# Attention and a mixture of experts on one core: small moves at attention's outer steps, a context load moved, and the experts' bounds read later

## The chip, the core and the metric

The kernel runs on one NeuronCore of a Trainium2 chip. A core has a matrix engine (TensorE, PE in the profile, with its weight loads as PEld), VectorE (DVE), ScalarE (ACT), GpSimd (POOL) and SyncE (SP), which here only issues transfers. The engines run on their own and wait for each other by semaphores. PSUM is the memory that TensorE writes; names that begin with `ps` are tiles in it. The metric is the device time of one execution in microseconds; lower is better.

## The reference, cut to what matters

The batch is 4, the sequence 1024, the width 1024, the context 1024 rows of 512. There are 32 experts with inner width 512, and each token goes to 4 of them. All tensors are float32.

```python
def _L0_xattn_ref(teacher_logits, teacher_features, Wq, bq, Wk, bk):
    query = jnp.einsum('bnc,dc->bnd', teacher_features, Wq) + bq
    key = jnp.einsum('bnc,dc->bnd', teacher_features, Wk) + bk
    energy = jnp.einsum('bnd,bmd->bnm', query, key)
    attention = jax.nn.softmax(energy, axis=-1)
    return jnp.einsum('bln,bmn->blm', teacher_logits, attention)
...
def _L0_ffn_ref(hidden_states, gate_w, gate_b, w_gate, b_gate, w_up, b_up, w_down, b_down):
    logits = x @ gate_w.T + gate_b
    topk_logits, topk_idx = jax.lax.top_k(logits, K)
    topk_weight = jax.nn.softmax(topk_logits.astype(jnp.float32), axis=-1)
    ...
    gate = jax.lax.ragged_dot(xt, w_gate, group_sizes) + b_gate[gid]
    up = jax.lax.ragged_dot(xt, w_up, group_sizes) + b_up[gid]
    gate = jnp.minimum(gate, SWIGLU_LIMIT)
    up = jnp.clip(up, -SWIGLU_LIMIT, SWIGLU_LIMIT)
    glu = gate * jax.nn.sigmoid(SWIGLU_ALPHA * gate)
    outs = jax.lax.ragged_dot((up + 1.0) * glu, w_down, group_sizes) + b_down[gid]
    ...
x = x + _L0_xattn_ref(_layernorm(x, axis=-1), ctx_1024, L0_xattn_Wq, L0_xattn_bq, L0_xattn_Wk, L0_xattn_bk)
x = x + _L0_ffn_ref(_layernorm(x, axis=-1), ...)
```

## The kernel before, in words

The program has two stages with a barrier between them: attention with routing (to about 640 us of the span), and the experts (to the end). Every large product is made of three float16 passes (high by high, high by low, low by high part), so that the result is close to float32. The order of the work on each engine is written out by hand; nothing is planned by a program.

**Attention.** Per batch, the context (2 MB, `cx`) is transposed in four pairs of tiles (`context`, L634), and the queries and keys are made from it in four quarters (`one_quarter`, L640), which VectorE reads out of PSUM with their bias (`queries_and_keys`, L850). Then there are eight tiles of 128 rows. `energies` (L609) fills `psE`; VectorE takes the row maximum (L860), ScalarE the exponent (L538); VectorE and ScalarE write the high and low parts of the probabilities (L545, L877) and of the normalised rows of x, and SyncE transposes both with DMA (L424, L429). A batch's second product (`product`, L676: 48 matmuls of 512 columns per tile, two halves of 24) runs one batch later than its energies. `schedule` lays out steps `step(s, b1, b2, more)`: b1 is the batch whose energies are made, b2 the one whose second product is made, s the tile, and `more` is False where b1 is past the last batch. So batch 0's energies stand alone (b2 is None), and the last batch's product stands alone (from `more` False at s = 0 and 1, then b1 None). I call these the outer steps; `both` is the step between them, in which the small matmuls (transposes of the second norm's rows L614, routing logits L623 into `psR`) stand between the large ones of the product.

In an outer step of the last batch TensorE makes the first half of the product, then 8 transposes into `psT`, 12 matmuls of the second half, the 8 logits matmuls, the last 12, and the two rank matmuls (L731, L732). The logits read `x2T`, which ScalarE copies out of `psT` (L578). The product goes to `psM` or `psE`: before, `psE` only where b1 is None and s is odd. VectorE adds the residual from it (L936).

**Between the stages** SyncE loads the first slot list (`idxg`, L457), GpSimd gathers the first 128 rows by it (`xg`, L510), and the barrier follows. SyncE also loads the first pieces of weights (`load_chunk`, L117).

**Experts.** Tokens are sorted into slots of 128 rows; an expert has 3 or more such tiles, and its last may be a half tile of 64 rows (`half_step`). Per tile, TensorE makes the gate product (`psG`, L1326), the transposes of the previous tile's activation (L1339), the up product (`psU`), the transposes of the next tile's rows (`psX`, L1332), and the previous tile's down product (`psY`, L1350): 24 matmuls each. After a half tile the down product is made in pairs of 64 rows that run together. ScalarE copies `psX` to `xT` (L1166) before the gate product can begin. The number of tiles is known only on the chip: an expert's first tile, its end of full tiles and its end are read into registers (`start_of` L1082, `full_end_of` L1085). `expert` reads all three at its start, behind the first tile's step of that expert, which the expert before has already issued.

```python
            def expert(e, par, last=False):
                t0, tf, t1 = start_of(pe, e), full_end_of(pe, e), start_of(pe, e + 1)
                ...
                with pe.Fori(t0 + 1, tf) as i:
                    step(i, e, par, False)
                with pe.If(t1 > tf):
```

## Time and profile before

| | |
|---|---|
| time, median of 3 runs | 3005.17 us (2998.52 to 3007.32) |
| time of the profiled execution | 3001.28 us |
| its span, first to last instruction | 2999.4 us |
| PE busy | 2887.7 us (96%) |
| DVE busy | 1705.9 us (57%) |
| ACT busy | 1193.8 us (40%) |
| POOL busy | 568.0 us (19%) |
| HBM traffic over the span | 156 GB/s |

The profile is one execution. Busy shares are of the span, and PE's leaves 112 us in which TensorE has nothing to do; the rows below say where they lie. The slices of the page show them at the start (0 to 100 us) and at the seam of the stages (600 to 675 us); elsewhere every slice is at 90% or more, but for the last.

### The profile page before, as it was taken

To read this page: it belongs to the slowest core of one execution; us is meant where nothing else is said; L and a number is where in the kernel's file an instruction comes from. 1 tells how busy PE (TensorE), PEld (TensorE's weight loads), DVE (VectorE), ACT (ScalarE), POOL (GpSimd) and SP (SyncE) were. 2 spreads that over 40 slices of the span, in tenths; PEclk is the share of its full clock that TensorE was granted. 3 is DMA by queue.
4 is the path that set the end of the run, shared out by engine and by line. 5 is a ranking of instruction groups with operands and counts; after the bars stand their busy time and mean duration, and the time that the engine had idled before them with its cause. 6 is when DMAs were issued, how large, how long until landed. Compare 5 with 4: busy or idle time off the path is not lost.

```text
span 2999.4 us, 44819 instructions
## 1 busy us (share of the span) xinstructions
PE 2887.7 (96%) x14948; PEld 1488.7 (50%) x14949; DVE 1705.9 (57%) x2552; ACT 1193.8 (40%) x1221; POOL 568.0 (19%) x502
## 2 busy tenths in 40 slices
PE   6899999959999999999999999999999999999997
PEld 3455555535454454444545444444544444455453
DVE  5887888654635454656554556655554654653532
ACT  3343333223524434544443445534444443442422
POOL 1132333321111111111111111211111111111111
PEclk8999999979999999999999999999999999999999
DMA  7977766555655555566755656766555665664433
GB/s 220 224 209 180 189 169 176 184 172 151 186 144 161 161 161 161 165 182 192 217 133 133 212 167 168 210 210 168 165 166 159 168 166 161 168 192 126 84 64 64
DMA packets 343547, 501.47 MB, mean 167 GB/s; under 512 B 190881, under 2 KB 190881, under 8 KB 343234
## 3 DMA queue, kind: packets, MB, share of 16 engines
q0 software_dynamic: 45856, 152.33, 22.9%
q10 hardware_dynamic: 94576, 225.46, 21.5%
q1 hardware_dynamic: 203058, 122.94, 15.9%
q8 instruction: 33, 0.54, 0.1%
q14 instruction: 24, 0.20, 0.0%
HBM read 354.64 MB, written 112.46 MB: 156 GB/s over the span
## 4 chain that ended last, share of the span: by engine, by line
PE 74%; DMA 2%; issue 1%; ACT 0%; DVE 0%; ACTq 0%; SPq 0%; POOL 0%; POOLq 0%; DVEq 0%
PE psY L1350 23%; PE psG L1326 22%; PE psU L1326 21%; PE psX L1332 4%; PE psG L1397 3%; PE psA L1339 2%; DMA acc<-y,idxs 1%; DMA idxs<-slots 1%; DMA bias<-in_L_ffn_b_down 0%; ACT y L1176 0%; ACT W L1073 0%; DVE y L1248 0%; SPq L1095 0%; ACT xT L1166 0%; ACTq L1092 0%
## 5 line engine op out<-in xcount | busy, mean ns | idle before, releaser
L1350 PE MATMUL psY<-W,aT 128*128 128x512 f16 (+1 forms) x3456 | 728.5, 379 | 3.0 <-DVE y L1248 3.0
L1326 PE MATMUL psG<-W,xT 128*128 128x512 f16 x3072 | 685.2, 379 | 16.6 <-issue 10.7
L1326 PE MATMUL psU<-W,xT 128*128 128x512 f16 x3072 | 684.1, 379 | 0.0
L1350 PEld LDWEIGHTS psY<-W,aT 128*128 128x128 f16 (+1 forms) x3456 | 321.1, 99 | 355.9 <-ACT aT L1170 3.3
L1326 PEld LDWEIGHTS psG<-W,xT 128*128 128x128 f16 x3072 | 299.7, 98 | 383.6 <-issue 21.3
L1326 PEld LDWEIGHTS psU<-W,xT 128*128 128x128 f16 x3072 | 299.3, 98 | 334.8
L1133 POOL DMA_INDIRECT acc<-y,idxs x143 | 229.4, 1604 | 1090.2 <-DVE y L1248 944.5
L1248 DVE SCALAR_TENSOR_TENSOR y<-psY,idxs,y 128x1024 f32<-128x1024 f32 x127 | 163.0, 1284 | 412.1 <-ACT y L1176 412.1
L676 PE MATMUL psM<-W,XT 128*128 128x512 f16 x1392 | 356.1, 379 | 5.8 <-DVE xr L936 5.2
L1176 ACT ACTIVATE y<-bias,idxs 128x1024 f32<-128x1024 f32 x143 | 164.3, 1149 | 464.5 <-DMA idxs<-slots 464.4
L1166 ACT ACTIVATE xT<-psX 128x1024 f32<-128x1024 f32 x145 | 148.3, 1023 | 461.7 <-PE psX L1332 436.6
L1128 POOL DMA_INDIRECT xg<-xn_tab,idxg x145 | 156.4, 1078 | 860.9 <-PE psX L1332 806.5
L1273 DVE SCALAR_TENSOR_TENSOR up<-psU,bias 128x512 f32<-128x512 f32 (+1 forms) x144 | 99.6, 692 | 278.5 <-PE psU L1326 278.0
L1262 DVE SCALAR_TENSOR_TENSOR gt<-psG,bias 128x512 f32<-128x512 f32 (+1 forms) x144 | 99.4, 690 | 261.1 <-PE psG L1326 205.2
L1078 DVE SCALAR_TENSOR_TENSOR W<-stage,W 128x2048 f16<-128x2048 f32 x93 | 212.4, 2284 | 9.1 <-ACT W L1073 9.1
L676 PEld LDWEIGHTS psM<-W,XT 128*128 128x128 f16 x1392 | 150.6, 111 | 126.9 <-DVE xr L936 6.9
L1078 DVE SCALAR_TENSOR_TENSOR W<-stage_more,W 128x2048 f16<-128x2048 f32 x93 | 212.4, 2284 | 1.2 <-ACT W L1073 1.2
L1170 ACT ACTIVATE aT<-psA 128x512 f32<-128x512 f32 x144 | 85.2, 592 | 263.5 <-PE psA L1339 255.8
L1073 ACT ACTIVATE W<-stage_more 128x2048 f16<-128x2048 f32 x93 | 176.3, 1896 | 34.7 <-issue 28.3
L1073 ACT ACTIVATE W<-stage 128x2048 f16<-128x2048 f32 x93 | 176.4, 1897 | 6.1 <-issue 5.9
L501 POOL DMA_INDIRECT slots<-pack,dest x128 | 138.2, 1079 | 200.1 <-DVE tok L912 162.3
L1332 PE MATMUL psX<-ident,xg 128*128 128x128 f32 x1160 | 152.1, 274 | 14.5 <-PEq L144 14.5
(170 smaller groups left out, 2616.7 us busy)
## 6 DMA issues: line engine op xcount, KB each, us to landing
stage_more<-in_L_ffn_w_down ACTq DMA_DIRECT2D x62, 1024.0 KB, 7.6
stage<-in_L_ffn_w_gate ACTq DMA_DIRECT2D x60, 1024.0 KB
stage_more<-in_L_ffn_w_up ACTq DMA_DIRECT2D x31, 1024.0 KB, 5.5
stage<-in_L_ffn_w_up ACTq DMA_DIRECT2D x30, 1024.0 KB
stage<-in_x SPq DMA_DIRECT2D x32, 512.0 KB
xr<-in_x SPq DMA_DIRECT2D x32, 512.0 KB
acc<-xr SPq DMA_DIRECT2D x32, 512.0 KB
xn_tab<-x2h SPq DMA_DIRECT2D x32, 512.0 KB
```

Of the source, the lines that this page charges most:

```text
L501: pool.indirect_dma_start(out=slots[:, :], out_offset=bass.IndirectOffsetOnAxis(dest[:, n % 2, k:k + 1], 0), in_=pack[:, n % 2, k, :], in_ ...
L676: op = pe.matmul(out[:, h * HALF:(h + 1) * HALF], XT[:, a, k, t * P:(t + 1) * P], AT[:, par(bk), c, k, h * HALF:(h + 1) * HALF].rearrange( ...
L1073: act.activation(W[:, par, HI, c * CHUNK:(c + 1) * CHUNK], slot(c), ACT.Copy, scale=S_W).then_inc(s_whi, 1)
L1078: dve.scalar_tensor_tensor(out=W[:, par, LO, c * CHUNK:(c + 1) * CHUNK], in0=slot(c), scalar=S_W, in1=W[:, par, HI, c * CHUNK:(c + 1) * CH ...
L1128: pool.indirect_dma_start(out=xg[:], out_offset=None, in_=xn_tab[:, :], in_offset=bass.IndirectOffsetOnAxis(idxg[:, 0:1].bitcast(U32), 0)) ...
L1133: pool.indirect_dma_start(out=acc[:, :], out_offset=bass.IndirectOffsetOnAxis(idxs[:, 0:1].bitcast(U32), 0), in_=y[:], in_offset=None, com ...
L1166: act.activation(xT[:].rearrange("p k q a -> p (k q a)").bitcast(F32), psX[:], ACT.Copy).then_inc(s_xTev, 1)
L1176: act.activation(y[:], bias[:, par, 2 * I:], ACT.Copy, scale=idxs[:, 1:2].bitcast(F32)).then_inc(s_y0, 1)
L1248: dve.scalar_tensor_tensor(out=tile_y[:], in0=psY[:], scalar=weight, in1=tile_y[:], op0=ALU.mult, op1=ALU.add).then_inc(s_y, 1)
L1326: op = pe.matmul(ps[:], xT[:, k, :, a], weights(par, c, offset + k * I, I), start=k == 0 and n == 0, stop=k == KH - 1 and n == 2)
L1332: op = pe.transpose(psX[:, n * P:(n + 1) * P], xg_w[:, n * P:(n + 1) * P], ident[:])
L1350: return pe.matmul(psY[at_row:at_row + rows, h * HALF:(h + 1) * HALF], aT[:, k, 0:rows, a], weights(par, c, 2 * KH * I + k * H + h * HALF, ...
```

## The change

- The first batch's context is loaded in four transfers of 0.5 MB, each with its own semaphore, and each pair of transposes waits for its own.
- Batch 2's context is loaded at step 1 of the next batch, behind the load of a residual tile, instead of at step 6 of batch 0.
- In batch 0's last step VectorE reads batch 1's queries and keys right after the low parts of tile 6, ahead of the statistics and the low parts of tile 7.
- At s = 0 and 1 of the last batch's product the outer step follows the rule of the others: odd tiles go to `psE`, and the product waits for the residual of the tile before the last one. In all of these steps the logits matmuls stand between those of the second half of the product, from its fifth on.
- At the seam SyncE loads the first slot list ahead of one piece of weights (w_up, stage slot 2), and ScalarE's copy of `xT` comes first, then the bias loads, then three loads of weights; before, the weights came first, then the bias, then the copy.
- In the experts' stage TensorE reads an expert's end behind its loop of full tiles. For an even expert the next one's end of full tiles is read there too, and the odd expert reads nothing at its start.

```diff
+            def load_first_ctx(pair):
+                rows = ctx_in[0, pair * 2 * P:(pair + 1) * 2 * P, :]
+                sp.dma_start(cx[:, 2 * pair:2 * pair + 2, :], rows.rearrange("(t p) c -> p t c", p=P)).then_inc(s_ctx0[pair], 16)
+
-            load_ctx(0)
+            for pair in range(NT // 2):
+                load_first_ctx(pair)
...
                 if b1 is not None:
+                    if s == 1 and b2 is not None and batch(b1) == 1:
+                        sp.wait_ge(s_cT, NT)
+                        load_ctx(2)
                     guarded(sp, more if s < 2 or s >= NT - 2 else None, next_x1)
                     guarded(sp, more if s < 2 else None, transposes)
-                    if s == NT - 2:
-                        guarded(sp, None if first(b1) else b1[0] < B - 3, next_ctx)
+                    if s == NT - 2 and not first(b1):
+                        guarded(sp, b1[0] < B - 3, next_ctx)
...
-                    if b1 is None:
+                    if b1 is None and s < NT - 1:
                         sp.wait_ge(s_wlo, s - 1)
                         g["load_chunk"](sp, 0, s - 2 + RING)
...
             sp.dma_start(g["idxg"][:], slots[0:P, :]).then_inc(g["s_idxg"], 16)
+            sp.wait_ge(s_wlo, NT - 2)
+            g["load_chunk"](sp, 0, NT - 3 + RING)
...
-        def product_of(s, b1):
-
-            return psE if b1 is None and s % 2 else psM
+        def product_alone(s, b1, more):
+
+            return b1 is None or s < 2 and more is False
+
+        def product_of(s, b1, more):
+
+            return psE if product_alone(s, b1, more) and s % 2 else psM
...
-                if pair == 0:
-                    alone(pe, s_ctx, per(16, bk, 16), s_past)
+                if first(bk):
+                    pe.wait_ge(s_ctx0[pair], 16)
+                elif pair == 0:
+                    pe.wait_ge(s_ctx, per(16, bk, 0))
...
-                    if b1 is None and s > 2:
+                    if product_alone(s, b1, more) and s > 0:
                         pe.wait_ge(s_exp, B * NT)
                         pe.wait_ge(s_x2, tile(b2, s - 1))
...
+                def logits_beside(m):
+                    if m == 4:
+                        pe.wait_ge(s_x2Tev, tile(bt, n + 1))
+                        if n >= 1 or not first(bt):
+                            pe.wait_ge(s_lgev, tile(bt, n))
+                    if 4 <= m < 4 + KH:
+                        logits_block(m - 4)
+
                 if b2 is not None and s < NT:
-                    product(product_of(s, b1), b2, s, 1, range(KH // 2))
-                if late:
-
-                    pe.wait_ge(s_x2Tev, tile(bt, n + 1))
-                    if n >= 1 or not first(bt):
-                        pe.wait_ge(s_lgev, tile(bt, n))
-                    for k in range(KH):
-                        logits_block(k)
+                    product(product_of(s, b1, more), b2, s, 1, range(KH // 2), logits_beside if late else None)
+                elif late:
+                    for m in range(4, 4 + KH):
+                        logits_beside(m)
...
                     if b2 is None and s > 0:
                         lo_parts(s - 1)
+                    if b2 is None and s == NT - 1:
+                        queries_and_keys(following(b1))
...
+            evac_x(0)
+            load_bias(act, 0, 0)
             for c in range(RING, NCHUNK):
                 load_chunk(act, 1, c)
-            load_bias(act, 0, 0)
-            evac_x(0)
...
-            def expert(e, par, last=False):
-
-                t0, tf, t1 = start_of(pe, e), full_end_of(pe, e), start_of(pe, e + 1)
+            def expert(e, par, known=None, last=False):
+
+                t0, tf = known or (start_of(pe, e), full_end_of(pe, e))
...
                 with pe.Fori(t0 + 1, tf) as i:
                     step(i, e, par, False)
+                t1 = start_of(pe, e + 1)
+                following = (t1, full_end_of(pe, e + 1)) if par == 0 else None
                 with pe.If(t1 > tf):
```

**VectorE, batch 0's last step.** `mx` is the row maximum of the last tile, `ah` and `xnh`/`xg` are the low parts, `stage<-ps..,bqk` the four readings of batch 1's queries and keys, BN_STATS the statistics of the tile's rows. Before:

```order
L860 TENSOR_REDUCE mx<-psE 128x1 [waits energy_done]
L861 TENSOR_SCALAR nmx<-mx 128x1 [waits softmax_chain]
L877 SCALAR_TENSOR_TENSOR ah<-stage,sc,ah 128x1024 [waits prob_scale_ready,prob_hi]
L880 SCALAR_TENSOR_TENSOR xnh<-stage,xnh 128x1024 [waits ln1_hi]
L821 BN_STATS st<-stage 128x6 [waits x1_in1]
L821 BN_STATS st<-stage 128x6
L823 BN_AGGR mv<-st 128x2 [waits ln1_chain]
```

Now, with the change:

```order
L881 TENSOR_REDUCE mx<-psE 128x1 [waits energy_done]
L882 TENSOR_SCALAR nmx<-mx 128x1 [waits softmax_chain]
L900 SCALAR_TENSOR_TENSOR ah<-stage,sc,ah 128x1024 [waits prob_scale_ready,prob_hi]
L903 SCALAR_TENSOR_TENSOR xnh<-stage,xnh 128x1024 [waits ln1_hi]
L871 TENSOR_SCALAR stage<-psM,bqk 128x512 [waits qk_done]
L871 TENSOR_SCALAR stage<-psQ,bqk 128x512 [waits qk_done]
L871 TENSOR_SCALAR stage<-psM,bqk 128x512 [waits qk_done]
L871 TENSOR_SCALAR stage<-psR,bqk 128x512 [waits qk_done]
L842 BN_STATS st<-stage 128x6 [waits x1_in1]
```

The four readings moved ahead of the statistics; before they came seven instructions later, behind the low parts of tile 7.

**TensorE, the last batch's product at s = 1.** `xs` are the normalised rows whose transposes go to `psT`, `psR` the logits, `psQ` the ranks. Before:

```order
L676 MATMUL psM<-W,XT 128x512 [waits ln1T_in1,x2_ready]
L676 MATMUL psM<-W,XT 128x512 x23
L614 MATMUL psT<-ident,xs 128x128 [waits ln2_ready]
L614 MATMUL psT<-ident,xs 128x128 x7
L676 MATMUL psM<-W,XT 128x512 x12
L623 MATMUL psR<-gateT,x2T 128x32 [waits logits_read,ln2T_evacuated]
L623 MATMUL psR<-gateT,x2T 128x32 x7
L676 MATMUL psM<-W,XT 128x512 x12
```

Now (the pair of a product's and a logits matmul goes on until there are eight logits):

```order
L693 MATMUL psE<-W,XT 128x512 [waits ln1T_in1,x2_ready,exp_done]
L693 MATMUL psE<-W,XT 128x512 x23
L629 MATMUL psT<-ident,xs 128x128 [waits ln2_ready]
L629 MATMUL psT<-ident,xs 128x128 x7
L693 MATMUL psE<-W,XT 128x512 x4
L638 MATMUL psR<-gateT,x2T 128x32 [waits logits_read,ln2T_evacuated]
L693 MATMUL psE<-W,XT 128x512
L638 MATMUL psR<-gateT,x2T 128x32
L693 MATMUL psE<-W,XT 128x512
```

The product's tile changed from `psM` to `psE`, and the wait of the logits for `x2T` (ln2T_evacuated) now stands behind 4 matmuls of the second half, before behind 12.

**TensorE's sequencer, from an even expert to its loop of full tiles and out of it.** Each TENSOR_LOAD reads a bound into a register. Before, the odd expert's start (the branch waits for that expert's weights):

```order
L1421 UNCONDITIONAL_BRANCH [waits weights_lo]
L1082 TENSOR_LOAD tile_start
L1082 ISA x2
L1085 REGISTER_ALU
L1085 TENSOR_LOAD full_end
L1085 ISA x2
L1082 ISA
L1082 TENSOR_LOAD tile_start
L1082 ISA x2
L1416 ISA
```

Now, behind the last full tile's down product of the even expert:

```order
L1373 MATMUL psY<-W,aT 128x512 x23
L1439 REGISTER_ALU
L1439 COMPARE_AND_BRANCH
L1105 ISA
L1105 TENSOR_LOAD tile_start
L1105 ISA x2
L1108 REGISTER_ALU
L1108 TENSOR_LOAD full_end
L1108 ISA x2
L1443 COMPARE_AND_BRANCH
```

The three reads at the odd expert's start are gone; the even expert has two at its end (and two instead of three at its start), the odd one has one.

## Rows read from the trace of the kernel before

**Rows 1.** Waits of PE from 640 us: us in total, times, longest us.

```profile
PE psG L1326 <- issue: 10.7, 15, 1.2
PE psG L1326 <- ACT xT L1166: 5.9, 3, 3.1
```

**Rows 2.** Timeline, start: start us, us, instruction, count [idle before <-releaser].

```profile
14.06 1.94 PE L634 MATMUL psM<-ident,W 128*128 128x128 f32 x8 [7.67 <-DMA W<-in_ctx]
...
21.56 7.13 PE L640 MATMUL psM<-W,WT 128*128 128x512 f32 x16 [1.11 <-ACT W L521]
```

**Rows 3.** Timeline, batch 0's last steps and the turn to batch 1.

```profile
83.26 1.98 PE L609 MATMUL psE<-stage 128*128 128x512 f32 x4 [1.48 <-ACT stage L538]
...
88.83 3.47 SPq L424 DMA_TRANSPOSE W<-ah  x1
...
89.85 1.28 DVE L821 BATCH_NORM_STATS2 st<-stage 128x6 f32<-128x512 f32 x2
...
95.58 0.74 DVE L850 TENSOR_SCALAR stage<-psM,bqk 128x512 f32<-128x512 f32 x1
96.12 8.89 SPq L424 DMA_TRANSPOSE W<-ah  x1
...
98.44 3.49 PE L609 MATMUL psE<-stage 128*128 128x512 f32 x4 [6.33 <-DVE stage L850]
101.77 10.82 PE L676 MATMUL psM<-W,XT 128*128 128x512 f16 x48
```

**Rows 4.** Timeline, the last batch's product at s = 0 and 1, and s = 3.

```profile
511.31 2.75 PE L676 MATMUL psM<-W,XT 128*128 128x512 f16 x12
...
511.51 1.02 ACT L578 ACTIVATE x2T<-psT 128x1024 f32<-128x1024 f32 x1 [1.40 <-PE psT L614]
...
513.90 1.87 PE L623 MATMUL psR<-gateT,x2T 128*128 128x32 f32 x16
...
518.20 0.30 PE L731 MATMUL psQ<-mask,before 128*128 128x32 f32 x2
...
519.75 5.35 PE L676 MATMUL psM<-W,XT 128*128 128x512 f16 x24 [1.03 <-DVE xr L936]
...
547.57 5.34 PE L676 MATMUL psE<-W,XT 128*128 128x512 f16 x24
```

**Rows 5.** Timeline of PE, a step that has logits between the product's matmuls.

```profile
434.24 0.38 PE L676 MATMUL psM<-W,XT 128*128 128x512 f16 x1
...
434.60 0.38 PE L676 MATMUL psM<-W,XT 128*128 128x512 f16 x1
```

**Rows 6.** Timeline, the seam of the two stages.

```profile
635.63 0.96 POOL L501 DMA_INDIRECT slots<-pack,dest  x1 [0.31 <-issue]
...
639.03 0.38 SPq L117 DMA_DIRECT2D stage<-in_L_ffn_w_up  x1
639.59 0.38 SPq L457 DMA_DIRECT2D idxg<-slots  x1
644.65 0.98 POOL L510 DMA_INDIRECT xg<-xn_tab,idxg  x1 [8.05 <-DMA idxg<-slots]
...
650.18 1.94 PE L1332 MATMUL psX<-ident,xg 128*128 128x128 f32 x8 [14.47 <-PEq L144]
...
655.22 6.66 PE L1326 MATMUL psG<-W,xT 128*128 128x512 f16 x24 [3.09 <-ACT xT L1166]
```

**Rows 7.** Transfers of the same slot list's kind: KB each, median us to landing.

```profile
idxs_last<-slots SPq DMA_DIRECT2D x1, 2.0 KB, 2.4
```

**Rows 8.** Reads of an expert's bounds, 812.7 to 815 us: ns min/median/max, start us.

```profile
L1082 PEldq TENSOR_LOAD <-tile_start x2: 298/298/299, 812.8 to 814.3; - x2
```

**Rows 9.** Timeline of PE, two experts' starts behind a half tile.

```profile
811.43 2.78 PE L1350 MATMUL psY<-W,aT 128*64 128x512 f16 x24
815.38 5.34 PE L1326 MATMUL psG<-W,xT 128*128 128x512 f16 x24 [1.17 <-issue]
...
926.67 5.34 PE L1326 MATMUL psG<-W,xT 128*128 128x512 f16 x24 [0.49 <-issue]
```

More of the change, by code:

```diff
@@ L230, in attention_and_routing @@
         s_ctx = sem("ctx_in")
+        s_ctx0 = [sem(f"first_ctx_in{pair}") for pair in range(NT // 2)]
         s_past = sem("waits_passed")
@@ L757, in step @@
                     inputs_landed(b2, s, 0)
-                    product(product_of(s, b1), b2, s, 0, range(KH))
+                    product(product_of(s, b1, more), b2, s, 0, range(KH))
                     inputs_landed(b2, s, 1)
@@ L784, in step @@
                 if b2 is not None and s < NT:
-                    product(product_of(s, b1), b2, s, 1, range(KH // 2, KH)).then_inc(s_xm, 1)
+                    product(product_of(s, b1, more), b2, s, 1, range(KH // 2, KH)).then_inc(s_xm, 1)
                 if b1 is not None:
@@ L935, in step @@
                     dve.wait_ge(s_xm, tile(b2, s + 1))
-                    dve.scalar_tensor_tensor(out=xr[:, s % 2, :], in0=product_of(s, b1)[:], scalar=1.0 / (S_ROWS * S_PROB),
+                    dve.scalar_tensor_tensor(out=xr[:, s % 2, :], in0=product_of(s, b1, more)[:], scalar=1.0 / (S_ROWS * S_PROB),
                                              in1=xr[:, s % 2, :], op0=ALU.mult, op1=ALU.add).then_inc(s_x2, 1)
@@ L943, in step @@
                         g["cut_lo"](dve, 0, 0, s - 3)
-                if b1 is not None and s == NT - 1:
+                if b1 is not None and b2 is not None and s == NT - 1:
                     guarded(dve, more, lambda: queries_and_keys(following(b1)))
@@ L1422, in expert @@
                     then(P)
+                return following
             pe.sem_inc(s_Y, 1)
@@ L1428, in _ @@
             with pe.Fori(0, PAIRS - 1) as pair:
+                known = None
                 for par in range(2):
-                    expert(pair * 2 + par, par)
-            expert(E - 2, 0)
-            expert(E - 1, 1, last=True)
+                    known = expert(pair * 2 + par, par, known)
+            known = expert(E - 2, 0)
+            expert(E - 1, 1, known, last=True)
 _INS = ["x", "ctx_1024", "L0_xattn_Wq", "L0_xattn_bq", "L0_xattn_Wk", "L0_xattn_bk", "L0_ffn_gate_w", "L0_ffn_gate_b",
```

## The prediction, made before the changed kernel ran

> **What bounds the kernel now.** I read the page first: TensorE is busy for 96% of the span, so a change pays where TensorE stands still or where its own work shrinks. Then I read the waits of PE, to see who ends its idle time. In the experts' stage the largest group, 10.7 us in 15 waits before the gate product, ends by "issue": no other engine is late there [rows 1]. Then the timeline at each place that the edits touch: the start [rows 2], the turn from batch 0 to batch 1 [rows 3], the last batch's product [rows 4], the seam of the stages [rows 6], and two experts' starts [rows 9]. Each is taken below as a time on TensorE's path, and I ask what is late next.
>
> **Start.** TensorE waits 7.67 us for the whole context and begins at 14.06; four groups of transposes and their copies later, at 21.56, the queries and keys begin: 7.5 us [rows 2]. With the load in four pieces, the last piece lands about when the whole did, and the first three groups are done by then. What stays is one group, 1.94, and the wait for its copy, 1.11 [rows 2]: 3.05 instead of 7.5, so 4.5 us saved. Three further issues on SP delay the loads behind them, which are wanted only after the queries and keys. Upper bound 5.1 (the group at full clock: the eight transposes of 0.11 us instead of 0.24 each), lower bound 0, if four small transfers land so much later than one large one.
>
> The Trainium skill, page "DMA: Bandwidth & Descriptors", section "Bandwidth", says to batch transfers to 1 MiB or more, with 2.0 us of fixed cost in its fit. By that, charged to each piece one after the other, the last would land some 6 us later and the start would lose 1.5 us (an estimate from the page). The trace of before has only the one large load here and does not settle it; the fixed cost should overlap when issues follow each other, so I keep the 4.5.
>
> **The turn to batch 1.** Before, the statistics of tile 7 begin at 89.85, the readings of the new queries and keys only at 95.58, and TensorE, idle since 98.44 - 6.33 = 92.11, makes the first energies at 98.44 [rows 3]. Now three readings run from about 90, and the fourth right after 92.11 and ends at 92.9 (0.74 each, [rows 3]): energies at 93.1, 5.3 us earlier. What is late next is tile 7's probabilities. Its statistics start at 92.9 instead of 89.85, so everything behind them moves 3.1 us back. Before, the two low parts ended where the readings began, at 95.58, and the probabilities' one, which the transpose needs, one pass or about 1.1 us sooner, at 94.5; now 97.6. Before, SP was at the context load then: it issued the transpose at 96.12 and took 8.89 us, against 3.47 for the tile before [rows 3]. With the context load gone it is through at 97.7 + 3.5 = 101.2 instead of 105.0. The product's 48 matmuls lasted 10.82, only 0.45 over 48 of 0.216, so its second half began at 107.1, 2.1 us after that issue was through [rows 3]. Now: 103.3, 3.8 us earlier, with a new wait of TensorE of 3 us between the halves (100.1 to 103.3), released by the transpose. Moving the context load back to step 1 costs the same 5.4 us of SP there, but the transposes and loads behind it are for tiles a full step and more away, and the context itself (about 10 us to land) has the whole of step 1; I cost it at 0, and at 3 if it lands after the first transposes of step 2.
>
> The clock takes some of it back: the four passes of a tile's energies took 3.49 us after the idle 6.33, and 1.98 after an idle 1.48 [rows 3], so after long idle time TensorE runs at 1.2 instead of 2.4 GHz. The 3 us hole may cost a few us of half clock, at half their length. I take 0.7, bounds 0 and 1.7 (8 matmuls at twice 0.216). So 3.1 us here, between 1 and 5.
>
> The page "TensorE: Matmul & The Clock Gate", section "HAM oscillation", of the Trainium skill says that idle gaps between bursts return the clock to half. The slow energies agree with that. By the rule at its worst the turn would give 2.1 us instead of 3.1.
>
> **Last batch's product.** At s = 1 and s = 2 the product waits for VectorE to read `psM`: 1.03 us each, of the same kind. The rank matmuls start at 518.20 and the product at 519.75, 1.55 later; four rank passes need some 0.35 of that. At s = 3, in the other PSUM tile, there is no wait [rows 4]. So 2 x 1.2 = 2.4 us saved. Next late would be the normalised rows for the transposes; the steps from s = 3 on already run at this pace. Bounds 1.5 and 2.4.
>
> **Logits joined to the product.** Apart, the cluster of logits costs 1.71: it starts at 513.90, behind 12 matmuls from 511.31 (12 x 0.216 = 2.6), and lasts 1.87 less the overlap of its end [rows 4]. Joined, product plus logits take 0.36 per pair [rows 5] against 0.216 alone: 8 x 0.14 = 1.14 us. That looks like 0.57 saved in each of eight steps. But the logits need `x2T`, which is ready at 512.53 [rows 4], and they now stand behind 4 matmuls, at 511.31 + 0.86 = 512.17. So 0.4 to 0.5 of waiting comes in, and the first logits pair, its weights not yet loaded, costs some 0.1 more: 1.7 against 1.7. I cost the eight steps at 0, bounds -3 (copy late when ScalarE is busy) and +4.5 (8 x 0.57). This edit is the most visible in the code, and I expect nothing of it.
>
> **Seam.** The slot list is issued at 639.59, behind a 1 MB load issued at 639.03, and the gather that waits for it starts at 644.65 [rows 6]: 5.1 us for 2 KB. A load of the same size elsewhere lands in 2.4 [rows 7]. The last scatter of slots is issued at 635.63 [rows 6]; I take about 2 us for its landing, so the list goes out at 637.8 and the gather at 640.2. That is 4.4 us earlier; sharing the queues with the 1 MB load, now issued while the gather runs, costs 0.1 at least and up to 2. I take 4.3, bounds 2 and 5. Then ScalarE's copy: the transposes end at 652.12, and the gate product starts at 655.22 after an idle 3.09 [rows 6], since ScalarE issues six transfers first. A copy of that size takes 1.02 [rows 4], with its two hand-overs 1.3: 1.8 saved. The bias, no longer behind 3 MB of weights, lets VectorE and ScalarE start tile 0 earlier, and of the remaining 2.8 us of waits for `xT` [rows 1] I take 0.6. The gate product at the seam ran its first matmuls at half clock (6.66 for 24, against 5.34 in [rows 9]); starting 2 us closer to the idle stretch can cost 0.5. Sum 4.3 + 1.8 + 0.6 - 0.5 = 6.2.
>
> **Experts.** The loss is behind half tiles only. A down product of 64 rows, run in pairs, is over in about 2.6 us (12 x 0.216), and the gate product could follow at 811.43 + 2.6 = 814.0; it starts at 815.38, so 1.3 is lost, 1.17 of it as idle time [rows 9]. Of the 15 waits [rows 1], seven are such, at even experts (0.97 to 1.17), and an eighth of 1.0 is put down to `xT`; six are of 0.49, at odd ones, and the last two experts have 0.5 and 0.15. TensorE's sequencer is then still reading bounds: one at 812.8, the third at 814.3 [rows 8], so 0.75 each. Odd experts lose 0.49 of idle [rows 9] and about 0.17 that the modelled ends hide, as do all the others. Now the even ones save one read, 8 x 0.75 = 6.0; the odd ones everything, 6 x 0.66 = 4.0; the last two 0.95; in one even case `xT` is ready only halfway, less 0.3. Sum 10.7, bounds 8 and 12. The reads come back behind the loop of full tiles, two at even experts and one at odd ones, up to 1.6 us, and what hides them is a down product at full length, 24 x 0.216 = 5.2. Three reads behind such a product leave no idle time today: all 15 waits are behind half tiles.
>
> **Sum.** 4.5 + 3.1 + 2.4 + 0 + 6.2 + 10.7 = 26.9. The profiled execution took 3001.28 (span 2999.4): 2974.4. The median of the runs is 3.9 above it: 2978.3. I say 2976.
>
> **Rivals.**
> (a) Only what lies behind no transfer pays: four pieces land late, the transpose holds the turn, the gather is slowed. Then experts 10.7, outer steps 2.4, 1.8 of the seam: 14.9, 2989 by the same mean. For it: all three rest on landings that the trace of before does not show. Against: 3.47 against 8.89 and 5.1 against 2.4.
> (b) The logits joined do gain 0.57 a step, 4.5 in all: 2971.5. Against it stands the 512.53 of `x2T`.
> (c) Slower: the reads behind the loop are not hidden. The price is 16 x 2 x 0.75 at even and 15 x 0.75 at odd experts, 35 us, against 26.9 of gain: 3011. It decides from when the sequencer is less than about 2.4 us ahead of TensorE at the end of a full down product (1.6 of reads and the branches). Against it: with three reads, 2.25 us, there is no gap behind full products.
> (d) The gaps are filled but the time is not: another engine is at its pace right behind. 3000. Against it: DVE and ACT are far from full in the experts' stage.
>
> **Numbers.** Chances: forecast 0.62, (a) 0.18, (b) 0.10, (c) 0.04, (d) 0.06. The likeliest's own range, from the bounds of its terms not all at one end, is 2968 to 2984. With (a) and (b) and the spread of 9 us between the runs shown: 2964 to 2990. About 0.3%, 9 us, is what can be told from no change. Faster 0.90, within 0.06, slower 0.04.
>
> **What would show it.** Right: TensorE's queries and keys begin near 17; the first energies of batch 1 run 5 us earlier in their turn, and a new wait of TensorE on `W<-ah` stands in the product's middle; waits before the product on `xr` vanish at s = 1 and 2; each logits cluster gone but a new wait on `x2T` of 0.4; the gather at the seam within 5 us of the last scatter; "issue" before the gate product under 4 us in all. Wrong: issue gaps in front of the transposes L1339 or the gate product behind full tiles, context transposes of batch 2 that wait for their load, or queries and keys still at 21.

## The result and the profile after

The changed kernel takes **2974.06 us** (median of 6, 2973.77 to 2975.55), against 3002.64 (median of 6) for the kernel before: ratio 0.9904, 95% interval 0.9892 to 0.9917. The forecast was 2976. The profiled execution has a span of 2972.2 us, 27.2 below the one before; the sum of the prediction was 26.9. That total is closer than its terms, so they are read one by one below.

The waits of TensorE from the seam on (us in total, times, longest), which answer to [rows 1]:

```profile
PE psX L1355 <- PEq L144: 11.1, 1, 11.1
PE psY L1373 <- DVE y L1271: 2.9, 2, 2.7
PE psG L1349 <- ACT xT L1189: 2.9, 3, 1.2
PE psG L1349 <- issue: 1.8, 7, 0.4
```

"Issue" has shrunk from 10.7 to 1.8 us, xT from 5.9 to 2.9, and nothing new has come in. The start, beside [rows 2]:

```profile
7.79 1.94 PE L651 MATMUL psM<-ident,W 128*128 128x128 f32 x8 [1.28 <-DMA W<-in_ctx]
...
12.81 1.04 PE L651 MATMUL psM<-ident,W 128*128 128x128 f32 x8
15.01 7.13 PE L657 MATMUL psM<-W,WT 128*128 128x512 f32 x16 [1.16 <-ACT W L536]
```

The last group of transposes starts at 12.81, though the last piece of the context had landed at 12.0: TensorE was still at the third group. Unlike the first two it runs at full clock (1.04 us). The queries and keys start 6.55 us earlier than before. The turn to batch 1, beside [rows 3]:

```profile
86.98 1.96 PE L624 MATMUL psE<-stage 128*128 128x512 f32 x4 [0.94 <-DVE stage L871]
88.78 5.34 PE L693 MATMUL psM<-W,XT 128*128 128x512 f16 x24
...
91.45 3.25 SPq L434 DMA_TRANSPOSE W<-ah  x1
...
96.21 5.34 PE L693 MATMUL psM<-W,XT 128*128 128x512 f16 x24 [2.10 <-DMA W<-ah]
```

The hole before the first energies is gone (0.94 instead of 6.33), a new one of 2.10 stands in the middle of the product, and the transpose takes 3.25 instead of 8.89. The long one has moved with the context load: at 114.18, 1.8 us behind that load, a transpose takes 9.62 us, and TensorE does not wait for it. The last batch's product, beside [rows 4]:

```profile
494.31 5.35 PE L693 MATMUL psM<-W,XT 128*128 128x512 f16 x24 [0.50 <-issue]
...
501.65 0.41 PE L638 MATMUL psR<-gateT,x2T 128*128 128x32 f32 x2 [0.25 <-ACT x2T L593]
507.56 5.34 PE L693 MATMUL psE<-W,XT 128*128 128x512 f16 x24
```

The wait on `xr` of 1.03 is gone at s = 1 (and at s = 2), and the first joined logits wait 0.25 for `x2T` in seven of the eight steps, 0.37 in the last. The seam, beside [rows 6]:

```profile
621.92 0.96 POOL L516 DMA_INDIRECT slots<-pack,dest  x1 [0.30 <-issue]
...
624.10 0.33 SPq L470 DMA_DIRECT2D idxg<-slots  x1
625.32 0.38 SPq L117 DMA_DIRECT2D stage<-in_L_ffn_w_up  x1
626.10 0.98 POOL L525 DMA_INDIRECT xg<-xn_tab,idxg  x1 [3.22 <-DMA idxg<-slots]
...
633.05 1.94 PE L1355 MATMUL psX<-ident,xg 128*128 128x128 f32 x8 [11.05 <-PEq L144]
```

The gather starts 4.18 us after the last scatter instead of 9.02, but TensorE's wait falls only from 14.47 to 11.05. The experts' starts behind a half tile, an even and an odd one, beside [rows 9] (a group that the view's window cuts shows fewer than 24 matmuls):

```profile
792.66 2.78 PE L1373 MATMUL psY<-W,aT 128*64 128x512 f16 x24
795.87 4.48 PE L1349 MATMUL psG<-W,xT 128*128 128x512 f16 x20 [0.42 <-issue]
...
903.88 2.78 PE L1373 MATMUL psY<-W,aT 128*64 128x512 f16 x24
906.59 5.35 PE L1349 MATMUL psG<-W,xT 128*128 128x512 f16 x24
```

At the odd one the gate product now follows 2.71 after the down product's start, with no idle time; at even ones 0.2 to 0.4 is left.

### The profile page after: what moved, and what is told of

It reads as the page before. It is cut to its first block, busy times and chain, and to the rows that moved or that the text cites. A ratio compares the mean times of both kernels' runs of the same rounds, so it can differ in the third digit from the quotient of the medians.

```text
span 2972.2 us, 44771 instructions
## 1 busy us (share of the span) xinstructions
PE 2885.2 (97%) x14948; PEld 1487.7 (50%) x14949; DVE 1705.2 (57%) x2552; ACT 1192.0 (40%) x1221; POOL 563.8 (19%) x502
## 3 DMA queue, kind: packets, MB, share of 16 engines
q10 hardware_dynamic: 94576, 225.46, 21.6%
## 4 chain that ended last, share of the span: by engine, by line
PE 76%; DMA 1%; ACT 0%; issue 0%; DVE 0%; SPq 0%; POOL 0%; ACTq 0%; POOLq 0%; DVEq 0%
PE psY L1373 23%; PE psG L1349 22%; PE psU L1349 22%; PE psX L1355 4%; PE psG L1420 3%; PE psA L1362 2%; DMA acc<-y,idxs 1%; DMA idxs<-slots 1%; ACT y L1199 0%; DVE y L1271 0%; ACT xT L1189 0%; SPq L1118 0%; ACT W L1096 0%; POOL acc L1180 0%; PE psU L1421 0%
## 5 line engine op out<-in xcount | busy, mean ns | idle before, releaser
L693 PE MATMUL psM<-W,XT 128*128 128x512 f16 x1344 | 349.2, 379 | 5.8 <-DVE xr L959 2.9
```

The costliest lines, as they stand in the source:

```text
L693: op = pe.matmul(out[:, h * HALF:(h + 1) * HALF], XT[:, a, k, t * P:(t + 1) * P], AT[:, par(bk), c, k, h * HALF:(h + 1) * HALF].rearrange( ...
```

## The experiments

Twelve kernels ran. Times are medians of the runs; the kernel before, run beside each group, took 3004.07, 3001.87 and 3003.08, so medians of two groups compare to 1 or 2 us. Where less matters, the stretch of the trace that the edit touches decides. "Changed" is the changed kernel, 2974.06.

**bounds_only**: the kernel before with `t0, tf = known or (...)` and the reads of `t1` and of the next expert's bounds behind `Fori`, and nothing else of the change.

> The kernel before with the experts' bounds edit alone: an expert's end and the next one's bounds read behind the loop of full tiles. Theory (the reads hide under a down product at full length, and what was lost was exposed behind half tiles): the waits of the gate product on issue, 10.7 us in 15 waits in the kernel before, fall under 2 us as in the changed kernel, and from the second gate product of the stage to the last down product TensorE gains 9.9 us, as the changed kernel did there: a span near 2989.5, ratio 0.9967. Rival 1 (the gain there was owed to the other edits, through the seam and the bias): a gain of 5 us or less. Rival 2 (the reads come back behind full tiles): new gaps before the activation's transposes, span at or above 2999.

2990.20 (4 runs), ratio 0.9950 (0.9934 to 0.9967). Waits of PE from 650 us:

```profile
PE psG L1326 <- ACT xT L1166: 4.5, 3, 2.6
PE psY L1350 <- DVE y L1248: 2.9, 1, 2.9
PE psG L1326 <- issue: 1.7, 7, 0.4
```

From the stage's second gate product to the last down product it takes 2300.3 us, the kernel before 2310.5, the changed kernel 2300.7. So the bounds edit alone is the whole gain of this stage, 10.3 us; rivals 1 and 2 fall. The medians differ by 13.9, with 5.8 between this kernel's own runs; the stretch is the better measure.

**more_reads**: four further `full_end_of(pe, e)` ahead of the read of `t1`.

> The changed kernel with four more reads of a bound behind each expert's loop of full tiles (six at even experts, five at odd ones; 0.75 us each). Theory (TensorE's sequencer is some 17 matmuls or 3.5 us ahead of the engine at the end of a full down product, and no more): 4.5 us of reads and the branch leave some 1.2 us exposed at 16 even experts, 3.75 us leave some 0.5 at 15 odd ones: 27 us more, between 15 and 40, as waits on issue before the activation's transposes or the gate product. Rival 1 (the whole down product of 5.2 us is cover): no more than 3 us. Rival 2 (reads behind the loop are never covered): 31 x 3.0 = 93 us more, and the changed kernel should already have shown it.

2995.40 (6 runs), 21.3 above changed; the stretch took 2323.0, 22.3 more. At even experts the hole comes behind a full down product, or before the half tile's transposes (7 waits of up to 0.9 us):

```profile
717.81 5.34 PE L1373 MATMUL psY<-W,aT 128*128 128x512 f16 x24
724.25 1.02 PE L1349 MATMUL psG<-W,xT 128*128 128x512 f16 x4 [1.10 <-issue]
...
1049.99 5.34 PE L1349 MATMUL psG<-W,xT 128*128 128x512 f16 x24 [0.88 <-issue]
```

Both rivals fall, and 22.3 lies within the theory's 15 to 40. From the start of the down product to what follows it takes 5.18 us where nothing is late. Here it takes 6.2 to 6.3 at most even experts, about 1.05 more, and 5.4 to 5.5 at odd ones, about 0.3 more; of the latter nearly nothing shows as idle time. That is 16.8 us and 4.3 us of the 22.3; 1.7 more is a late gather at the stage's third tile, which no read causes; the rest is small and goes both ways. The reads are a little shorter than the 0.75 that was expected: behind the product at 717.81 the first starts at 719.4 and the last ends near 723.5, 4.1 us for six, and five take 3.4. So 4.1 - 1.05 and 3.4 - 0.3 both leave about 3.1 us of reads covered, less than the product's 5.2 and less than the 3.5 of the theory. The changed kernel uses 1.5 of it.

**logits_apart**: all logits in a cluster again.

```diff
-                    product(..., range(KH // 2), logits_beside if late else None)
-                elif late:
+                    product(..., range(KH // 2))
+                if late:
```

> The changed kernel with the eight logits of a step in a cluster of their own again, behind the first half of the down product's second half, in all steps that the joining touched. Theory (joining was worth about nothing, since x2T comes 0.25 us later than the first joined pair wants it): the outer steps take 0 to 0.6 us more over eight steps, and the time is that of the changed kernel within 1 us, 2974 to 2975. Rival (joining gained 0.57 a step, and the 0.25 wait was there anyway): 4.5 us more, 2978.5.

2976.12 (4 runs, 2974.34 to 2976.34), 2.1 above changed, just outside the 2974 to 2975 of the theory and in doubt by as much. The trace is sharper: step after step takes 13.30 us apart and 13.24 joined, which is 0.06 a step, 0.4 in all. Its profiled execution has a span of 2972.6, 0.4 above changed, although it lost 1.7 to a half clock at the last batch's first product (below), which changed did not. So the theory holds in the trace, and the rival's 4.5 falls.

**logits_later**: `at = 6 if b1 is None else 4`, the logits beside matmuls `at` to `at + 7`. As b1 is None only from s = 2 on, the edit reaches six of the eight steps and not all, as the expectation has it.

> The changed kernel with the joined logits of the last batch's steps beside matmuls 6 to 13 of the second half of the product instead of 4 to 11, so that x2T, late by 0.25 us, is ready. Theory (the wait costs TensorE its 0.25 us in each of eight steps): the wait on x2T is gone and the steps' period of 13.24 us falls to 12.99, 2.0 us in all: 2972. Rival (the period is set by the chain over VectorE and the wait only moves, to the rank matmuls or the product on xr): period still 13.24 and 2974.

2973.27 (4 runs, 2970.36 to 2977.53). Two steps of changed, and two of this kernel:

```profile
541.38 0.41 PE L638 MATMUL psR<-gateT,x2T 128*128 128x32 f32 x2 [0.25 <-ACT x2T L593]
...
554.62 0.41 PE L638 MATMUL psR<-gateT,x2T 128*128 128x32 f32 x2 [0.25 <-ACT x2T L593]
```

```profile
546.04 0.39 PE L638 MATMUL psR<-gateT,x2T 128*128 128x32 f32 x2
...
558.86 0.39 PE L638 MATMUL psR<-gateT,x2T 128*128 128x32 f32 x2
```

The step takes 12.82 instead of 13.24: the wait of 0.25 is gone, and 0.17 more than was expected, which the view does not explain (the ends of matmuls are modelled). At s = 0 and 1 the wait and the 13.24 are still there. From the last batch's first product to the seam's first transpose it takes 138.5 us against 138.7, and 1.7 of that is a half clock which changed does not have there: 1.9 us saved. The rival falls; the median cannot show it. Against the 13.30 of logits_apart the joined step now gains 0.48, near the 0.57 of rival (b): joining is worth that once `x2T` is no longer waited for.

**ctx_whole and ctx_eight**: batch 0's context in one load on one semaphore, and in eight loads `cx[:, t, :]`, each tile's transposes waiting for their own.

> The changed kernel with batch 0's context in one load of 2 MB instead of four of 0.5 MB; everything else stays. Theory (two things made the start: the pieces let three groups of transposes run during the load, and the pieces as such land 1.8 us sooner in all): the load lands near 13.8, the queries and keys start near 21.5, all 6.5 us are lost: 2980.6. Rival (the last piece landed at 12.0 only because the other loads were issued later): it would land near 13.8 too here, as those loads are issued early again; the next run tells these apart. Rival 2 (the start is hidden by batch 0's slow steps): less than 3 us lost.

> The changed kernel with batch 0's context in eight loads of 0.25 MB, one for each tile, and each tile's four transposes waiting for its own. Theory (fixed cost of a transfer overlaps when issues follow each other; what counts is bytes in front): the last piece lands at 12.0 plus or minus 0.5 and the queries and keys start at 14.1 to 15.0, 0 to 1 us sooner than with four. Rival (the rule that small transfers cost their fixed time each, 2.0 us by the Trainium skill, page DMA: Bandwidth & Descriptors; or the issue on SP, 0.4 to 0.6 us each, sets the pace): the last piece is issued some 2 us later and lands at 13.5 or later, and the start is 1 to 3 us slower than with four.

2979.73 (2 runs) and 2974.74 (2 runs). Their starts, whole first:

```profile
14.12 1.94 PE L651 MATMUL psM<-ident,W 128*128 128x128 f32 x8 [7.70 <-DMA W<-in_ctx]
...
20.98 7.13 PE L657 MATMUL psM<-W,WT 128*128 128x512 f32 x16 [1.16 <-ACT W L536]
```

```profile
11.60 1.04 PE L654 MATMUL psM<-ident,W 128*128 128x128 f32 x8
13.84 7.13 PE L660 MATMUL psM<-W,WT 128*128 128x512 f32 x16 [1.20 <-ACT W L536]
```

The start is worth 6.0 us in its place and 5.7 in the time. In these executions the last bytes land at 14.0 as one load (issued at 1.85), at 12.0 as four (the last issued at 3.34), at 11.4 as eight (the last at 5.16). The last load of each, with us from issue to landing:

```profile
W<-in_ctx SPq DMA_DIRECT2D x1, 2048.0 KB, 12.1
```

```profile
W<-in_ctx SPq DMA_DIRECT2D x1, 512.0 KB, 8.7
```

```profile
W<-in_ctx SPq DMA_DIRECT2D x1, 256.0 KB, 6.2
```

These landings vary from one execution to the next, and the other kernels' traces show by how much, as their starts have the same instructions. As one load the bytes were in at 13.1 to 14.0 (three executions), as four at 12.0 to 12.8 (nine), as eight at 11.4 and 11.8 (two). The queries and keys started at 20.8 to 21.6, at 14.8 to 16.0, and at 13.8 and 14.1. So more pieces did land sooner, but four against one is worth about 1 us and not always 2. The rate of the queues from 4 to 8 us does not explain it: 260 to 292 GB/s, 249 to 310, and 307 and 339. The other loads are issued later the more pieces there are, so that less competes may be a part of it; the run that would have held them back was not made, and the cause of the sooner landing stays open. The 1.2 us that eight pieces gain did not reach the end: batch 0's steps took 48.7 us from the first energies to the last, against 47.4 in changed. Five sets of energies behind idle times took 16.8 us there against 14.6, as more of them ran at half clock.

**turn_ctx_back and turn_reads_late**: one half of the turn's change undone in each, `load_ctx(2)` at `s == NT - 2` again, or `queries_and_keys` at the step's end again.

> The changed kernel with batch 2's context loaded at batch 0's last steps again, and VectorE's early readings of queries and keys kept. Theory (both edits are needed, the later of two waits ends it): the transpose of the probabilities takes about 9 us again behind the load, the second half of the first product starts 5 us later than in the changed kernel, and all of the turn's 5.0 us is lost: 2979. Rival (each edit has its own part): 2 to 3 us lost.

> The changed kernel with VectorE's readings of the new queries and keys at the end of batch 0's last step again, and batch 2's context still loaded later. Theory (both edits are needed): the first energies of batch 1 come 5.3 us later, the product behind them is held by them and not by the transpose, and all of the turn's 5.0 us is lost: 2979. Rival (each has its own part): 2 to 3 us lost.

2980.33 and 2980.67 (3 runs each), 6.3 and 6.6 above changed. The first:

```profile
85.65 1.96 PE L621 MATMUL psE<-stage 128*128 128x512 f32 x4 [0.94 <-DVE stage L868]
...
90.11 7.68 SPq L434 DMA_TRANSPOSE W<-ah  x1
...
99.88 7.45 PE L690 MATMUL psM<-W,XT 128*128 128x512 f16 x24 [7.09 <-DMA W<-ah]
```

and the second:

```profile
91.27 3.74 SPq L434 DMA_TRANSPOSE W<-ah  x1
...
94.01 3.75 PE L624 MATMUL psE<-stage 128*128 128x512 f32 x4 [6.34 <-DVE stage L871]
97.55 11.42 PE L693 MATMUL psM<-W,XT 128*128 128x512 f16 x48
```

Each half alone gives nothing. In their places the two took 7.1 and 5.8 us more than changed, from batch 0's last energies to the end of batch 1's first product. With the readings alone the transpose is still 7.68 us and the hole moves into the product (7.09, and 2.1 more at half clock); with the load alone moved, TensorE still waits 6.34 for the readings. The theory of both expectations holds, a little exceeded by the clock.

**list_behind, chunk_last and copy_behind**: the seam. The slot list's load behind the chunk load again; `sp.wait_ge(s_xg, 16)` ahead of the chunk load; ScalarE's chunks, bias and then `evac_x(0)` again.

> The changed kernel with the first slot list's load issued behind the 1 MB chunk load again. Theory: the list takes about 5 us from its issue to the gather instead of 2.0, the gather itself 4.4 instead of 5.8, the chunk load waits for VectorE's low part 1.2 us longer: last scatter to first transpose 14.5 us instead of 11.1, 3.4 us lost: 2977.5. Rival (the gather's order on the queues decides nothing, its 128 rows wait for the scatters anyway): under 1 us lost.

> The changed kernel with the 1 MB chunk load at the seam issued after the gather has landed instead of 0.8 us before it starts; the chunk is for expert 1 and is not used before tile 1. Theory (the gather took 5.8 us instead of 4.4 because the chunk load shared the queues): 4.4 us from the gather's issue to its landing, and the time from the last scatter to the stage's first transpose falls from 11.1 to 9.7 us. Rival (the gather is slower by itself right behind the scatters, whose writes are still under way): 5.8 us again, and no gain.

> The changed kernel with ScalarE's copy of the first transposed rows behind its loads again (three chunks, then the bias, then the copy). Theory: the first gate product waits 3.1 us instead of 1.2 for xT, the next expert tile's 1.8 instead of 1.1: 2.4 us lost in all, 2976.5. Rival (the six issues are done before the transposes end, since the gather is what everything waits for): nothing lost.

2978.65, 2975.23 and 2975.88 (2 runs each). In the same order:

```profile
627.79 0.51 SPq L472 DMA_DIRECT2D idxg<-slots  x1
632.80 0.98 POOL L525 DMA_INDIRECT xg<-xn_tab,idxg  x1 [7.93 <-DMA idxg<-slots]
638.24 1.94 PE L1355 MATMUL psX<-ident,xg 128*128 128x128 f32 x8 [14.26 <-PEq L144]
```

```profile
627.88 0.98 POOL L526 DMA_INDIRECT xg<-xn_tab,idxg  x1 [3.05 <-DMA idxg<-slots]
632.24 0.38 SPq L117 DMA_DIRECT2D stage<-in_L_ffn_w_up  x1
633.35 1.94 PE L1356 MATMUL psX<-ident,xg 128*128 128x128 f32 x8 [9.39 <-PEq L144]
```

```profile
634.27 1.94 PE L1355 MATMUL psX<-ident,xg 128*128 128x128 f32 x8 [11.24 <-PEq L144]
...
639.67 0.58 PE L1349 MATMUL psG<-W,xT 128*128 128x512 f16 x1 [3.46 <-ACT xT L1189]
```

TensorE's wait is 14.26, 9.39 and 11.24, against 11.05 in changed. The list's order gives 3.2, and the chunk load beside the gather takes 1.7 back: the gather lands 4.3 us after its issue without it, 5.8 with it. The executions agree: 4.1 to 4.4 in the five where the load is issued well before or after the gather, 5.6 to 6.1 in eight where it is issued 0.6 to 0.9 us ahead of it (in the ninth, more_reads, the trace has no landing). So chunk_last's rival falls: right behind the scatters the gather is as fast as elsewhere. The copy's order gives 2.25 (3.46 against 1.21), but the second tile's wait stays at 1.12 in copy_behind, so the 0.6 that I gave the bias is not owed to this order by itself. chunk_last's median is 1.2 above changed although its seam is shorter; its profiled execution lost 1.7 to half clock at 494, over 100 us ahead of the seam.

**combined**: chunk_last, logits_later and ctx_eight together.

> The changed kernel with three things added: the 1 MB chunk load at the seam issued after the gather has landed, the last batch's logits beside matmuls 6 to 13, and batch 0's context in eight loads. Theory: 1.4 us (the gather takes 4.4 us again instead of 5.8), 1.9 us (steps of 12.81 instead of 13.24 us, as logits_later showed in its trace) and 1.2 us (queries and keys at 13.8), 4.5 together: 2969.6, as TensorE has no other work there that could take their place. Rival (the start's and the steps' gains are taken back by stretches of half clock, which fall at other places in each arrangement and are worth 1 to 3 us): 2972 to 2974, with the same gains visible in the trace at their places.

2971.35 (4 runs, 2969.81 to 2972.16), ratio 0.9894 (0.9876 to 0.9911). The seam's wait is 9.42, the steps take 12.81, the queries and keys start at 14.1 (by the marks, 0.9 before changed). All three gains are at their places (0.9, 2.1 and 1.6), some 4.6 in sum, and 2.7 is left in the medians, between theory and rival. The trace has what the rival names: half clock costs 1.7 in the turn's second half product and 1.7 at the last batch's first one, where changed has full clock, and gives 1.7 back at the very last product. The ratio's interval overlaps that of the changed kernel, so that this version is faster than it is likely, not shown.

**The toss.** The same 24 matmuls, at the same place behind the same idle times, in changed, more_reads and chunk_last, which have the same instructions up to there:

```profile
494.31 5.35 PE L693 MATMUL psM<-W,XT 128*128 128x512 f16 x24 [0.50 <-issue]
```

```profile
496.19 6.97 PE L693 MATMUL psM<-W,XT 128*128 128x512 f16 x24 [0.50 <-issue]
```

```profile
494.58 7.04 PE L694 MATMUL psM<-W,XT 128*128 128x512 f16 x24 [0.50 <-issue]
```

At 2.4 GHz they take 5.3, with 1.7 more where some eight of them run at 1.2 (they start 0.43 us apart instead of 0.22). At this place 3 of the 14 profiled executions (before, bounds_only, changed) stayed at full clock. With two more that are also the same up to there, list_behind and copy_behind, the changed kernel's instructions got full clock in one execution of five. What decides it was not looked for. The very last down product ran in 5.34 in two, before and combined, and in 6.7 to 7.0 in the twelve others:

```profile
2951.58 7.00 PE L1373 MATMUL psY<-W,aT 128*128 128x512 f16 x24 [2.75 <-DVE y L1271]
```

## Why the prediction was right

Term by term, from marks in the two profiled executions, in us:

| place | predicted | measured |
|---|---|---|
| start | 4.5 | 6.55 |
| batch 0's steps | 0 | -0.5 |
| turn | 3.1 | 5.0 |
| batches between | 0 | -0.1 |
| last batch's steps, logits joined | 2.4 + 0 | 2.8 |
| seam, to the second gate product | 6.2 | 5.05 |
| experts, to the last down product | 10.7 | 9.9 |
| last down product at half clock | 0 | -1.7 |
| end | 0 | 0.2 |
| sum | 26.9 | 27.2 |

**The sum.** The mechanisms were right in every large term. That the sum came within 0.3 us is luck: the start and the turn gave 3.95 more than their terms and the logits 0.4, the seam, the experts, batch 0's steps and the last product 4.15 less. So is the median's part: I put 3.9 us between profile and median, from three runs; with six, the kernel before lies 1.4 above its profile and the changed one 0.1.

**Start.** The mechanism was right and the term too small, for two reasons. The pieces land sooner than the whole, so that the last group began at 12.81 instead of 14.06, 1.25; and that group with its copy took 2.20 instead of the 3.05 that I had worked out at half clock, 0.85. The pair of executions also flatters the change: over the three executions with one load the queries and keys started at 21.1 on average, over the nine with four at 15.3, 5.8 us sooner. The rule to batch transfers to 1 MiB or more (the Trainium skill, page "DMA: Bandwidth & Descriptors", section "Bandwidth") is one for the share of peak bandwidth. Charged to each piece as a time, by which the start would lose 1.5 us, it does not hold here: with 0.25 MB pieces the same 2 MB were in at 11.4 and 11.8 us instead of 13.1 to 14.0. My bound of 5.1 was wrong with it, since I let no case land sooner than the whole.

**Turn.** 3.8 less 0.7 for the clock was predicted. The transposing began 0.2 and was through 0.4 sooner than worked out, and its end released TensorE 1.5 us behind instead of 2.1; the clock cost nothing in this execution, and 1.7 in logits_later and combined, whose same second half took 7.03. So 0 and 1.7 were the true ends of that term, and that this execution had the cheap end is luck. The context load that I moved at a cost of 0 did cost nothing: the batches between lost 0.1, although SyncE spent 9.62 us in the transpose behind it. The two experiments show that the gain belongs to neither half of the edit alone, as the prediction's "what is late next" had it.

**Outer steps.** 14.51 became 13.30 with the cluster kept (logits_apart; the first of the two steps once the 1.7 of half clock is taken off), 1.21 each: the 2.4 are exact. The most visible edit, the joining, was costed at 0 and gave 0.4; the wait on `x2T` that I put against it is there, 0.25 long.

**Seam.** The list's term failed in size: 4.3 predicted, 3.4 came. The gather was issued 4.84 us earlier (predicted 4.4), but took 5.8 beside the chunk load, against 4.4 before: 1.4 lost, where I had put 0.1, with 2 as the bound. The copy gave 1.9 (predicted 1.8), and the half clock cost 0.9 (7.56 against 6.66 for the first 24 matmuls, predicted 0.5). The wait for the second `xT` fell by 0.65 (predicted 0.6), but as copy_behind shows, not by the order of bias and weights alone; which edit gave it stays open, and that it came in the size of the term is luck.

**Experts.** 9.9 of 10.7, and 10.3 in bounds_only. The even experts came as worked out: from the start of the half tile's down product to that of the gate product it took 0.75 to 0.80 less in seven of the eight, one read, and the 0.2 to 0.4 of idle time that is left there is what the term left. What was mis-sized is the odd experts: 0.55 each instead of 0.66 (3.27 became 2.72), so 3.3 instead of 4.0, since the modelled ends hide less there than the 0.17 that I added to the idle 0.49. The last two experts gave 0.8 instead of 0.95. Rival (c) had a real condition: it wanted a lead under 2.4 us. In more_reads the first read starts at 719.4, 3.6 us before the next matmul could (717.81 + 5.18), and 3.1 of reads are covered. Rivals (a), (b) and (d) fall: all three landings came, the gather's with a part of what (a) feared, joining gave 0.4 and not 4.5, and the filled gaps are time.

## What to carry to other kernels

Where TensorE is 96% busy, the gain lies in small holes, and a hole can have two late parties: undoing either half of the turn's edit cost 6.3 to 6.6 us of time, all of the 5.0 that both halves gave and some half clock. So ask, before filling a hole, who is late next. Ask what a small transfer stands behind, and then also what will share its time: moving the chunk load behind the list gave 3.2 us and left 1.7 beside the gather. And weigh gains of 1 to 2 us by the stretch of the trace that they touch, since the clock behind a hole can take or leave 1.7 us, which a median of two or four runs does not level. The same goes for landings: compare a transfer over every trace that has it, not over one pair.

## What was not expected of the hardware

- One load of 2 MB landed at 13.1 to 14.0 us, the same bytes as four loads at 12.0 to 12.8, as eight at 11.4 and 11.8.
- The same gather of 128 rows took 4.1 to 4.4 us, and 5.6 to 6.1 with a 1 MB load issued 0.6 to 0.9 us ahead of it.
- TensorE's sequencer covers about 3.1 us of register reads (0.65 to 0.75 each) behind a down product of 24 matmuls that lasts 5.2, and no more.
- A transpose of the probabilities held SP for 3.3 us in the median, never over 5.1 without a load just ahead of it, and for 8.7 to 9.6 with a 2 MB load issued 1.6 to 1.8 us ahead, 7.7 with one 3.0 ahead.
- The clock behind an idle stretch differs between executions of the same instructions (5.35 or 6.97 to 7.04 us for 24 matmuls).
